# Layer 2 attention with keys and values shared by all heads, and the heads' weights folded into queries and output

## What is computed

```python
scale = jnp.sqrt(jnp.float32(D_K))
q = z @ wq @ fcq_w + fcq_b          # wq: 128 -> 64, fcq_w: 64 -> 16 heads x 64
k = z @ wk @ fck_w + fck_b
v = z @ wv @ fcv_w + fcv_b
...
scores = jnp.einsum('bihd,bjhd->bhij', q, k) / scale
attn = jax.nn.softmax(scores, axis=-1)
out = jnp.einsum('bhij,bjhd->bihd', attn, v)
out = out.reshape(b, n, N_HEAD * D_V)
return out @ fco_w + fco_b
```

## Time and profile before

| | |
|---|---|
| time, median of 3 runs | 2787.68 us (2783.92 to 2794.81) |
| profiled execution, span (first to last instruction) | 2860.1 us |
| mean granted clock of TensorE | 0.930 of full speed |
| busy: PE / PEld / DVE / ACT / POOL | 89% / 57% / 64% / 46% / 43% |
| chain that ended last, by engine | PE 43%; DVE 5%; ACT 3% |
| L2055 maxima on DVE | 256 of 686 ns, 165.4 us |
| L2069 exponentials on ACT | 512 of 472 ns, 235.6 us |
| L2099 transposes on PE | 1024 of 280 ns, 160.6 us |
| L2107 copies of transposes on DVE | 128 of 681 ns (median) |

### The profile page before, as it was taken

One profiled execution on the slowest core, in us unless ns is written; L12 is line 12 of the kernel. 1 busy time (PEld: TensorE's weight loads), 2 busy tenths in 40 slices (PEclk: granted clock), 3 DMA queues, 4 the chain that ended last, 5 costly groups with the idle time before them and its releaser, 6 DMA issues.

```text
span 2860.1 us, 39521 instructions
## 1 busy us (share of the span) xinstructions
PE 2550.0 (89%) x13960; PEld 1617.9 (57%) x13960; DVE 1839.4 (64%) x3692; ACT 1323.6 (46%) x3393; POOL 1239.4 (43%) x1120
## 2 busy tenths in 40 slices
PE   6787799999999999979879999999999689897988
PEld 3475355555555555554445666666555358676766
DVE  5777467776776777656756777777665644656623
ACT  4575524434344243334445666665456224455433
POOL 2553267777677676743552333331000721233331
PEclk8799899999999999979999999999999778889888
DMA  4463200000000000009311222222101342212113
GB/s 167 141 204 111 99 1 1 1 1 1 1 1 1 1 1 1 1 4 241 92 38 53 68 67 68 67 64 57 30 1 46 90 133 48 55 42 57 40 40 96
DMA packets 186516, 159.27 MB, mean 56 GB/s; under 512 B 98336, under 2 KB 165344, under 8 KB 185504
## 3 DMA queue, kind: packets, MB, share of 16 engines
q1 hardware_dynamic: 163536, 90.70, 11.6%
q0 software_dynamic: 22784, 66.05, 7.4%
HBM read 126.94 MB, written 59.51 MB: 65 GB/s over the span
## 4 chain that ended last, share of the span: by engine, by line
PE 43%; DVE 5%; ACT 3%; issue 3%; another core or an unknown queue 1%; POOL 0%; DVEq 0%; ACTq 0%
PE bank L65 38%; PE bank L2099 4%; ACT L3298 1%; DVE work L2055 1%; DVE work L3360 0%; ACT weights_odd L3024 0%; DVE work L3412 0%; PE bank L2971 0%; DVE work L2032 0%; DVE work L3563 0%; PE bank L672 0%; DVE work L2107 0%; PE bank L3108 0%; DVE work L3528 0%
## 5 line engine op out<-in xcount | busy, mean ns | idle before, releaser
L1535 POOL TENSOR_TENSOR work<-work 128x512 f32<-128x512 f32 x384 | 488.7, 1273 | 299.9 <-DVE work L1527 280.1
L65 PE MATMUL bank<-work 64*128 64x256 f32 (+5 forms) x4384 | 593.7, 354 | 23.2 <-DVE work L3563 7.2
L65 PE MATMUL bank<-weights_odd,normed_channels 128*128 128x512 f32 (+2 forms) x1088 | 509.3, 575 | 53.1 <-DVE work L1527 52.6
L65 PEld LDWEIGHTS bank<-work 64*128 64x128 f32 (+4 forms) x4384 | 415.5, 172 | 225.5 <-issue 152.9
L1527 DVE TENSOR_TENSOR work<-bank,work 128x512 f32<-128x512 f32 x360 | 244.6, 687 | 112.7 <-PE bank L65 101.4
L2069 ACT ACTIVATE work<-bank,work 128x256 f32<-128x256 f32 x512 | 235.6, 472 | 159.9 <-DVE work L2055 153.2
L65 PEld LDWEIGHTS bank<-weights_odd,normed_channels 128*128 128x128 f32 x1088 | 176.1, 193 | 180.0 <-DVE work L1527 99.3
L2055 DVE TENSOR_REDUCE work<-bank 128x2 f32<-128x512 f32 x256 | 165.4, 686 | 173.5 <-PE bank L65 150.6
L599 POOL DMA_INDIRECT weights_even<-in_L_Wx,expert_slots x112 | 111.7, 998 | 339.9 <-PE bank L672 271.6
L1602 ACT ACTIVATE work<-bank,work 128x256 f32<-128x256 f32 x256 | 118.8, 469 | 295.4 <-DVE work L1589 295.1
L65 PE MATMUL bank<-work,weights_odd 128*128 128x512 f32 (+2 forms) x520 | 199.3, 505 | 25.0 <-ACT work L3323 9.0
(11 more groups left out here) (345 smaller groups left out, 4472.4 us busy)
## 6 DMA issues: line engine op xcount, KB each, us to landing
filter_matrices<-in_L_filters SPq DMA_DIRECT2D x24, 512.0 KB, 8.4
work<-filter_matrices SPq DMA_DIRECT2D x16, 768.0 KB
weights_even<-noted_rows SPq DMA_DIRECT2D x56, 132.0 KB
noted_rows<-in_empty SPq DMA_DIRECT2D x11, 660.0 KB, 10.5
noted_rows_in<-in_empty SPq DMA_DIRECT2D x8, 660.0 KB, 10.7
weights_odd<-noted_rows_in SPq DMA_DIRECT2D x40, 132.0 KB
...
```

The lines of the kernel that those rows point to most:

```text
L65: return pe.matmul(out, lhsT, rhs, start=first, stop=last, skip_group_check=True)
L1535: gp.tensor_tensor(self.sum_of(p), self.sum_of(p), self.product_of(p), ALU.add).then_inc(s["l1_add"], 1)
```

## The change

Keys and values are no longer formed for each head. For all heads alike, `zk = z wk` (64 numbers, laid down twice, once for each half of the partitions) and `zv = z wv` (64 numbers per token) are formed once for each group of tokens, in the head of the layer: `tensor_z` runs in the place of the router's logits, with one weight block `Wz` of 88 columns (8 logits, 16 shifts, 64 values) and one key product with `Wk`. The heads' key weights are multiplied onto the query weights beforehand (`Fq` = wq fcq_w fck_w^T per head) and the value weights onto the output fold (`Fvo` = fcv_w fco_w per head). That takes more and smaller joint products: 16 of 64x64, 32 with one column (64 rows), 8 with one column (128 rows), 16 of 64x128, two of 64x512 and four of 8 columns. Biases are carried along as columns (`q_bias`, `to_bias`, `both_b`).

In the loop the value products with their additions and the key products with theirs are gone; the query products stay in even slots, and the loop starts at slot -2 instead of -6, with three router steps in each of those two slots. The scores take the keys from `zk`, the products with the probabilities take `z`. What is constant over a row of the scores would drop out in the softmax; `vector_bias` still rounds the maximum as the full score would: for each unit VectorE subtracts a shift from the four maxima and adds it again, and the exponentials wait for the second of the two. ScalarE and GpSimd keep their orders; SyncE loads nine weight tensors as before, of other shapes.

The diff, cut to what the prediction speaks of:

```diff
+L2_Z = EXPERTS + L2_HEADS + L2_DH
...
+        self.Wq, self.Wk = take(P), take(P)
+        flat = [take(L2_PAIRS * L2_DH) for _ in range(3)]
+        self.FqT, self.FkT, self.FvT = [by_pair(a) for a in flat]
+        self.Fo = by_pair(take(L2_PAIRS * P))
+        c = take(3 * L2_PAIRS + 1)
+        self.cols, self.q_b, self.k_b, self.v_b, self.o_b = c, c[:, 0:8], c[:, 8:16], c[:, 16:24], c[:, 24:25]
+        self.Wz = take(L2_Z)
...
+        self.zk, self.z = work.take(TOKENS), work.take(TILES * L2_Z).rearrange("p (t w) -> p t w", w=L2_Z)
...
     def tensor_joint(self, pe, on):
         s, b = self.k.sem, self.k.bank[4:8]
+        halves = [slice(half * L2_DH, (half + 1) * L2_DH) for half in range(2)]
         on.wait_ge(s["l2_small"], self.SMALL)
-        for c in range(2):
-            for half in range(2):
-                r = slice(half * L2_DH, (half + 1) * L2_DH)
-                mm(pe, b[2 * c + half][:, :], self.Wqk[r, :], cols(self.Fqk, c)[r, :]).then_inc(s["l2_misc"], 1)
-        yield
-        for c in range(2):
-            on.wait_ge(s["l2_joint"], c + 1)
-            mm(pe, b[c][:, :], self.Wv[0:L2_DH, :], cols(self.Fv, c)[0:L2_DH, :]).then_inc(s["l2_misc"], 1)
-        yield
-    def tensor_logits(self, pe, on, g):
-        on.wait_ge(self.k.sem["l2_joint"], 3)
-        self.router.tensor_logits(pe, on, g)
+        for m in range(L2_PAIRS):
+            for r in halves:
+                last = mm(pe, b[0][r, m * L2_DH:(m + 1) * L2_DH], self.FqT[r, m, :], self.FkT[r, m, :])
+        last.then_inc(s["l2_joint_mm"], 1)
+        for m in range(L2_PAIRS):
+            for r in halves:
+                mm(pe, b[1][r, m:m + 1], self.FkT[r, m, :], self.q_b[r, m:m + 1])
+                mm(pe, b[1][r, L2_PAIRS + m:L2_PAIRS + m + 1], self.FqT[r, m, :], self.k_b[r, m:m + 1])
+        for m in range(L2_PAIRS):
+            last = mm(pe, b[1][:, 2 * L2_PAIRS:2 * L2_PAIRS + 1], self.Fo[:, m, :], self.v_b[:, m:m + 1], first=m == 0, last=m == L2_PAIRS - 1)
+        last.then_inc(s["l2_joint_mm"], 1)
+        yield
+        for m in range(L2_PAIRS):
+            for r in halves:
+                last = mm(pe, b[2 + m // 4][r, m % 4 * P:(m % 4 + 1) * P], self.FvT[r, m, :], self.Fo[r, m, :])
+        last.then_inc(s["l2_joint_mm"], 1)
+        yield
+        on.wait_ge(s["l2_joint"], 4)
+        for half, r in enumerate(halves):
+            last = mm(pe, b[half][:, :], self.Wq[r, :], self.joint[r, :])
+        last.then_inc(s["l2_joint_mm"], 1)
+        yield
+        on.wait_ge(s["l2_joint"], 6)
+        for half, r in enumerate(halves):
+            mm(pe, b[2 + half][:, 0:L2_PAIRS], self.Wq[r, :], self.to_bias[r, :])
+            last = mm(pe, b[2 + half][:, L2_PAIRS:2 * L2_PAIRS], self.k.ones[r, :], self.both_b[r, :])
+        last.then_inc(s["l2_joint_mm"], 1)
+        yield
     def vector_joint(self, v, on):
-        s, b = self.k.sem, self.k.bank[4:8]
-        for i in range(4):
-            on.wait_ge(s["l2_misc"], 4)
-            v.tensor_copy(cols((self.Fqk, self.Fk)[i % 2], i // 2), b[i][:, :]).then_inc(s["l2_joint"], 1)
-        yield
-        for c in range(2):
-            on.wait_ge(s["l2_misc"], 5 + c)
-            v.tensor_copy(cols(self.Fv, c), b[c][:, :]).then_inc(s["l2_joint"], 1)
-            yield
...
+    def tensor_z(self, pe, on, g):
+        k, s = self.k, self.k.sem
+        on.wait_ge(s["l2_joint"], self.JOINT)
+        on.wait_ge(s["ln_done"], GROUPS * self.n + g + 1)
+        on.wait_ge(s["l2_z"], 2 * (g - 1))
+        for i in range(TPG):
+            t = TPG * g + i
+            last = mm(pe, self.b_z[g % 2][:, i * L2_Z:(i + 1) * L2_Z], k.xn[:, t * P:(t + 1) * P], self.Wz)
+        last.then_inc(s["l2_z_mm"], 1)
+        mm(pe, self.b_keys[g % 2][:, :], self.Wk, cols(k.xn, g)).then_inc(s["l2_z_mm"], 1)
+    def vector_z(self, v, on, g):
+        s = self.k.sem
+        on.wait_ge(s["l2_z_mm"], 2 * g + 1)
+        v.tensor_copy(self.z[:, TPG * g:TPG * (g + 1), :], self.b_z[g % 2][:, 0:TPG * L2_Z].rearrange("p (t w) -> p t w", w=L2_Z)).then_inc(
+            s["l2_z"] if g < GROUPS - 1 else s["logits"], 1)
+        on.wait_ge(s["l2_z_mm"], 2 * g + 2)
+        v.tensor_copy(cols(self.zk, g), self.b_keys[g % 2][:, :]).then_inc(s["l2_z"], 1)
+    def vector_ahead(self, v, on):
+        yield from self.vector_joint(v, on)
+        for g in range(GROUPS):
+            self.vector_z(v, on, g)
+            yield
+    def vector_shift(self, v, on):
+        s = self.k.sem
+        on.wait_ge(s["logits"], self.router.nth + 1)
+        to = self.z[:, :, EXPERTS:EXPERTS + L2_HEADS]
+        v.tensor_tensor(to, to, self.shift.unsqueeze(1).to_broadcast([P, TILES, L2_HEADS]), ALU.add).then_inc(s["l2_shifted"], 1)
+    Z = 2 * GROUPS - 1
+    @staticmethod
+    def query_pair(slot):
...
-    def tensor_shared(self, pe, on, slot, kinds):
...
-    def vector_shared(self, v, on, slot, kinds):
...
+        return n if half == 0 and 0 <= n < L2_PAIRS * GROUPS else None
+    def tensor_query(self, pe, on, n):
+        s, (g, m) = self.k.sem, divmod(n, L2_PAIRS)
+        on.wait_ge(s["l2_q"], n)
+        mm(pe, self.b_misc[:, :], self.Fq[:, m * P:(m + 1) * P], cols(self.k.xn, g)).then_inc(s["l2_q_mm"], 1)
+    def vector_query(self, v, on, n):
+        s, m = self.k.sem, n % L2_PAIRS
+        on.wait_ge(s["l2_q_mm"], n + 1)
+        on.wait_ge(s["l2_score"], 4 * (n - 1))
+        v.tensor_scalar(self.q[n % 2], self.b_misc[:, :], self.q_bias[:, m:m + 1], L2_DH ** -0.5, ALU.add, ALU.mult).then_inc(s["l2_q"], 1)
...
-        q, kk = self.q[pair % 2][r, t], self.kk[pair % 2][r, t]
+        q, kk = self.q[pair % 2][r, t], cols(self.zk, g)[r, t]
...
     def vector_max(self, v, on, n, half):
         s, h = self.k.sem, 2 * n + half
         on.wait_ge(s["l2_score"], h + 1)
-        on.wait_ge(s["l2_exp"], 2 * (h - 7))
-        v.tensor_reduce(self.mx[h % 8][:, 0:2], self.b_score[h % 3][:, :].rearrange("p (i j) -> p i j", j=SEQ), AX.X,
+        on.wait_ge(s["l2_exp"], 4 * (n - 3))
+        v.tensor_reduce(self.mx[n % 4][:, 2 * half:2 * half + 2], self.b_score[h % 3][:, :].rearrange("p (i j) -> p i j", j=SEQ), AX.X,
                         ALU.max, negate=True).then_inc(s["l2_max"], 1)
+    def vector_bias(self, v, on, n):
+        s, (g, m, b) = self.k.sem, self.unit(n)
+        t = TPG * g + TPG // BPG * b
+        shift = self.z[:, t:t + 2, EXPERTS:EXPERTS + L2_HEADS].rearrange("p t (e m) -> p e t m", e=2)[:, :, :, m]
+        mx = self.mx[n % 4][:, 0:4].rearrange("p (e t) -> p e t", e=2)
+        on.wait_ge(s["l2_shifted"], 1)
+        on.wait_ge(s["l2_max"], 2 * n + 2)
+        v.tensor_tensor(mx, mx, shift, ALU.subtract).then_inc(s["l2_bias"], 1)
+        on.wait_ge(s["l2_bias"], 2 * n + 1)
+        v.tensor_tensor(mx, mx, shift, ALU.add).then_inc(s["l2_bias"], 1)
...
-        on.wait_ge(s["l2_max"], h + 1)
+        on.wait_ge(s["l2_bias"], 2 * n + 2)
...
-                h, r = 2 * m + half, half * L2_DH
-                c = slice((h % 8) * L2_DH, (h % 8 + 1) * L2_DH)
-                last = mm(pe, self.b_o[r:r + L2_DH, b * SEQ:(b + 1) * SEQ], self.v[2 * b + jc][h // 8][:, c],
+                r = half * L2_DH
+                last = mm(pe, self.b_o[r:r + L2_DH, b * SEQ:(b + 1) * SEQ], self.z[:, TPG * g + TPG // BPG * b + jc, EXPERTS + L2_HEADS:],
...
-        mm(pe, self.b_fo[:, :], self.Fo[:, m, :], self.o[pair % 2], first=m == 0, last=m == L2_PAIRS - 1).then_inc(s["l2_fold"], 1)
+        mm(pe, self.b_fo[:, :], self.Fvo[:, m, :], self.o[pair % 2], first=m == 0, last=m == L2_PAIRS - 1).then_inc(s["l2_fold"], 1)
...
-    FIRST, LAST = -6, L2_UNITS * GROUPS + 6
+    FIRST, LAST = -2, L2_UNITS * GROUPS + 6
...
-        self.norm.tensor(pe, on, self.tensor_joint(pe, on), self.tensor_logits)
-        on.wait_ge(s["l2_joint"], self.JOINT)
-        self.shared_free = [(s["route"], self.router.at + 1), (s["l2_joint"], self.JOINT)]
-        on.wait_ge(s["ln_done"], GROUPS * (self.n + 1))
+        self.norm.tensor(pe, on, self.tensor_joint(pe, on), self.tensor_z)
+        on.wait_ge(s["l2_z"], self.Z)
+        on.wait_ge(s["logits"], r.nth + 1)
         for slot in range(self.FIRST, self.LAST):
             for which, at in enumerate(self.COUNTS):
                 if slot == at:
@@ -2253,12 +2294,12 @@
             if (n := self.due(slot, 0)) is not None:
                 self.tensor_score(pe, on, n, 0)
                 self.tensor_score(pe, on, n, 1)
-            self.tensor_shared(pe, on, slot, ("v",))
             if (n := self.due(slot, 2)) is not None:
                 self.tensor_turn(pe, on, n, 0)
             if (n := self.due(slot, 3)) is not None:
                 self.tensor_times_v(pe, on, n)
-            self.tensor_shared(pe, on, slot, ("qk",))
+            if (n := self.query_pair(slot)) is not None:
+                self.tensor_query(pe, on, n)
...
-        self.norm.vector(v, on, self.vector_joint(v, on))
+        self.norm.vector(v, on, self.vector_ahead(v, on))
+        self.vector_shift(v, on)
```

(11 more changed lines are left out.)

133 lines of the change are left out of this document (52 added, 81 removed).

## The result

The changed kernel took 2754.4 us (median of 4 runs, 2752.8 to 2765.9) against 2785.8 for the kernel before (4 runs, 2777.7 to 2794.8): a ratio of 0.9903, 95% interval 0.9875 to 0.993. By the medians that is 31.4 us less, by the ratio 27. In a second comparison it was 2762.0 to 2784.9, ratio 0.9906 (0.9878 to 0.9935), 22.9 us less by the medians and 26 by the ratio. Forecast were 2756 us and 31.4 us less.

What follows compares the result with a forecast made beforehand. TensorE, full in units 32 to 103, was taken as the bound, with VectorE's copy right behind. The loop saves 44 us (29, 8, 3, 4), the head costs 12.6: 31.4 less than 2787.7, so 2756 us, own range 2740 to 2772.

Steps and rivals of the forecast that it cites:

- Odd slots, the key product saved and waited away again: Odd slots: without the key product (0.97 us) TensorE waits for VectorE's copy; slots of 5.92 or 6.83 become 6.01.
- parts 2 and 3: Odd slots: second transposes wait for VectorE's copy; the two small operations cost 0.41 us, so it ends at 3.46.
- Even slots unchanged: Even slots of units 32 to 103: query product stays, the copy is just in time, 5.27 us stays.
- Value products, 33 us in the tight window: Units 32 to 103: 36 of 72 slots lose a value product of 0.91 us on TensorE, 33 us.
- tight window: Units 32 to 103, 434.6 us with TensorE always busy; 36 pairs of slots at 11.28 make 406, 29 less.
- Units 12 to 31, 8 us: 12 value products save 11 us on an engine idle 28 of 146, less 10 even slots x 0.3; bounds 0 and 18.
- Units 0 to 11, 3 us gained: VectorE with the router's steps is last there and loses 2 us, TensorE a little more; bounds -2 and 8.
- The head, 12.6: Layer's head, longer: joint products +7, norm steps +7.6, a hole +3, shorter start of loop -5; bounds +7 and +22.
- The end: End of the loop: 8 value products save 7 us, less some 12 slots x 0.2 to 0.3: 4; bounds -1 and 8.
- (a): Loop: TensorE's full 120 us counts, the transposes find the bank free, odd slots fall to 5.0: 2716 us; chance 0.10.
- (b): Loop: the two small VectorE operations cost 0.9 us, odd slots 0.5 longer, even ones too: 2816 us; chance 0.13.
- (c): Head dearer at half clock, +22 instead of +12.6, and units 12 to 31 give nothing: 2774 us; chance 0.20.

Runs made afterwards that it cites:

- second pair: Changed kernel with the two small VectorE operations (subtract, add) done twice per unit: 2810.2 us, ratio 1.0095 to the kernel before; units 32 to 103 took 430.43 us.
- cross test: Changed kernel with odd slots' second transposes in the query's bank and a key-shaped product in every odd slot: 2748.7 us, ratio 0.9861 to the kernel before.
- third trace: Kernel before, unchanged, traced once more beside later runs: median 2784.2 us; units 12 to 31 took 106.25 us, units 32 to 103 took 433.72.
- key products back: Changed kernel with a product of the old key product's shape in every odd slot, result unused: 2833.7 us, ratio 0.9922 to the kernel before.
- first trace: Kernel before, unchanged, the profiled execution that the prediction read: 2860.1 us, 72 us longer than the median of its runs (2787.68).

## Why the prediction was right, step by step

**Odd slots, the key product saved and waited away again** (parts 2 and 3): right, the copy's end to the hundredth. Forecast were a copy's end at 3.46, 0.70 on TensorE and 1.85 behind it, 6.01; measured 3.46 and a slot of 5.91. What was 0.10 too long: the transposes start 0.14 behind the copy and the fold 0.46 behind them, 0.60 where the earlier trace rows, at another place, gave 0.70. The pair was put at 0.41 and costs 0.40. The idle time is 0.86 in each odd slot, for "about 1". The bank as the cause was shown by the cross test.

**Even slots unchanged:** 5.28 for 5.27. The working behind it ("the copy is just there") was right, too: of the second pair's 0.40 an even slot took 0.39.

**Value products, 33 us in the tight window:** the size is right (32.4 in all for 29), the name isn't. Put back alone the value products cost 16.4, the key products alone 0.0; in odd slots both stand before the same wait. The forecast came out because its sum was taken from whole slots, old against new (odd ones 6.83 and 5.92, now both 5.91), and not from the products.

**Units 12 to 31, 8 us:** 7.3 where VectorE doesn't stand still beside the scatters; on the other chip most likely nothing. In the trace that gives the 7.3, TensorE was full before (106.25 of 106.25); the reason given, an engine idle 28 of 146 us, belonged to a trace in which VectorE stood still. That the size fits is luck in part.

**Units 0 to 11, 3 us gained:** wrong, 1.5 lost. The step "VectorE with the router's steps is the last there" left out TensorE's clock. The first 10 us of this stage after, and in the third trace of the kernel before:

```profile
1345.48:1355.48 10.00, 8.47 (x27) 5.12 (x28) 6.88 (x16) 4.46 (x17) 7.54 (x8) 0.53 0.96 215
```

```profile
1321.97:1331.97 10.00, 8.55 (x48) 4.53 (x46) 8.80 (x19) 6.42 (x25) 9.39 (x11) 1.00 0.91 204
```

The clock is 0.53 where it was 1.00: TensorE had just idled 3.06 us ahead of the first scores, which wait for VectorE's query addition (L2064), behind its router steps. Over the whole stage it was 0.84, and 0.97 before. With the useless key products in it ("key products back"), this stage took 57.01 us at 1.00, so 4.5 less with more work. From reciprocal to reciprocal the two traces differ in four units: 0, 1, 6 and 9, in which the changed kernel was granted 0.50, 0.56, 0.79 and 0.88, took 0.7, 1.5, 1.6 and 0.8 us longer; the others agree within 0.3, one of them (8) even at 0.60. So the loss goes with the clock, and at 1.00 the forecast's 3 us are there (60.05 to 57.01). Why the clock came back sooner in that trace isn't shown: the same wait of 3.06 stands ahead of its first scores.

**The head, 12.6:** short by 1 to 3.6 us. By the events that the prediction used, the first maxima came 13.6 later behind the layer's start (1341.73 - 1286.22 against 1326.28 - 1284.40); to the first reciprocal, against the third trace, it is 16.2. Term by term: the joint products were 6.01 + 3.68 + some 1.9 = 11.6 for 11.5, but by two errors that cancel. The 64x128 ones cost twice what was put down (0.23, at half the clock), and the first turn took less than its 7.3, because the clock stood at 1.00 for some 3.4 us of it, which brought the records of one column from 55 down to 31 ns. With the clock at 0.50 throughout, the same turn took 8.84. So the head comes out near the forecast by luck in the clock: five of the ten traces with this head took 2.5 us more up to the norm steps. The norm steps grew from 2.61 to 3.47:

```profile
1308.94 1.12 PE L65 MATMUL bank<-weights_even,normed_channels 128*128 128x88 f32 x8 [2.46 <-DVE weights_even L2009]
...
1317.68 1.02 PE L65 MATMUL bank<-weights_even,normed_channels 128*128 128x88 f32 x8
...
1321.15 1.02 PE L65 MATMUL bank<-weights_even,normed_channels 128*128 128x88 f32 x8
...
1339.39 2.08 PE L65 MATMUL bank<-work 64*128 64x256 f32 x8 [3.06 <-DVE work L2064]
...
1341.73 1.28 DVE L2087 TENSOR_REDUCE work<-bank 128x2 f32<-128x512 f32 x2
```

8 x 0.86 = 6.9 for 7.6; the hole ahead of the first of them was 2.46 for 3. Up to the first step's product the head cost 8.8 and 9.9 more than in the third and the first trace of the kernel before, for 7 + 3 = 10. The eight steps and what follows them up to the first scores were to cost 7.6 - 5 = 2.6 and cost 5.1 against the third trace (30.45 for 25.35), 2.6 against the first, whose own clock was lower there (0.82 for 0.93). What was left out: the first scores run at half the clock (2.08), and the first exponentials now wait for both maxima and the pair, so from the maxima to the reciprocal it is 3.75 for 2.69.

The end gave 4.3 for 4. In all it is 26.4 us in the layer by the traces and 23 to 31 by the runs, for 31.4: the tight window gave 32.4 for 29 (a pair of slots took 11.15, where 11.28 were forecast), units 0 to 11 were 4.5 worse, and the head 3.6 dearer. The mechanism of the tight window is right and shown. That the medians differ by exactly 31.4 is luck: the second comparison gave 22.9, and the errors of the terms partly cancel. Rivals (a) and (b) are refuted at their size; of (c), the head went a third of the way to its +22 (16.2).
